# A transformer block in float32 parts: row maxima as one transpose a quad through device memory, and the relu output's high part on GpSimd

## The reference

```
qkv = layernorm(x) @ w_qkv.T + b_qkv           # 16 heads of 16
s   = (q * 0.25) @ k.T + mask                  # rows in 4 blocks of 128
a   = softmax(s) @ v
x1  = x + layernorm(a @ w_out.T + b_out)
h   = relu(layernorm(x1) @ W1 + b1)            # 1024 wide
out = x1 + layernorm(h @ W2 + b2)
```

## Time and profile before

| | us |
|---|---|
| median of 3 runs | 2275.53 (2271.7 to 2275.71) |
| the profiled execution, its own time | 2267.57 |
| its span, first to last instruction | 2265.8 |
| PE busy in the span | 2116.1 (93%) |
| DVE busy | 1567.3 (69%) |
| ACT busy | 1418.0 (63%) |
| POOL busy | 764.4 (34%) |

### The profile page before, as it was taken

How to read it: one execution, slowest core, us unless ns; L and a number is a source line. 1 busy time by engine, 2 the same in 40 slices (tenths; PEclk the granted TensorE clock), 3 DMA queues, 4 the chain that set the end, 5 groups by cost and what they waited for, 6 DMA issues and landing times.

```text
span 2265.8 us, 50967 instructions
## 1 busy us (share of the span) xinstructions
PE 2116.1 (93%) x18432; PEld 1648.0 (73%) x18432; DVE 1567.3 (69%) x3140; ACT 1418.0 (63%) x2437; POOL 764.4 (34%) x1161
## 2 busy tenths in 40 slices
PE   4899999999999999999999999999999999999985
PEld 2577777777777777777777777777777777777765
DVE  5767786667776677776667776677776667776542
ACT  2567666566666666666666666666666666666563
POOL 2033333233233233233233233243233233233234
PEclk8999999999999999999999999999999999999998
DMA  5332343332333323333323333322333323332300
GB/s 132 84 59 64 78 85 69 68 59 62 80 78 70 72 54 69 81 79 71 73 53 69 82 79 70 74 55 67 83 79 70 75 53 70 82 79 61 65 22 20
DMA packets 128931, 158.35 MB, mean 70 GB/s; under 512 B 27617, under 2 KB 78561, under 8 KB 128737
## 3 DMA queue, kind: packets, MB, share of 16 engines
q1 hardware_dynamic: 128208, 155.24, 32.0%
q10 hardware_dynamic: 528, 0.52, 0.1%
HBM read 37.17 MB, written 16.78 MB: 24 GB/s over the span
## 4 chain that ended last, share of the span: by engine, by line
PE 56%; DVE 15%; issue 10%; ACT 8%; POOL 6%; SPq 1%; DMA 1%; DVEq 0%; POOLq 0%; ACTq 0%
PE p_lin L341 17%; PE p_lin L445 14%; PE p_att L326 6%; POOL h_lo L678 5%; PE p_lin L377 5%; DVE neg_max L554 4%; PE p_lin L373 4%; PE p_att L323 4%; PE p_lin L334 3%; PE p_lin L386 2%; ACT h_hi L503 2%; ACT h_f L503 2%; DVE qk L569 2%; PE p_lin L403 2%; DVE x_lo L565 2%
## 5 line engine op out<-in xcount | busy, mean ns | idle before, releaser
L554 DVE TENSOR_REDUCE neg_max<-p_att 128x4 f32<-128x1024 f32 (+1 forms) x640 | 765.5, 1212 | 237.3 <-PE p_att L323 162.6
L472 ACT ACTIVATE probs<-p_att 128x1024 f32<-128x1024 f32 x640 | 635.7, 1027 | 253.6 <-PE p_att L326 158.0
L678 POOL TENSOR_TENSOR h_lo<-h_f,h_hi 128x256 fp32r<-128x256 f32 x512 | 365.1, 737 | 584.6 <-ACT h_hi L503 581.5
L503 ACT ACTIVATE h_f<-p_lin,b_s 128x256 f32<-128x256 f32 x512 | 249.2, 487 | 264.4 <-PE p_lin L341 264.4
L341 PE MATMUL p_lin<-x_hi,w_hi 128*128 128x256 f32 (+1 forms) x1280 | 304.6, 319 | 35.8 <-DVE x_lo L565 19.2
L326 PE MATMUL p_att<-stack 49*128 49x256 f32 (+1 forms) x3072 | 311.8, 304 | 9.6 <-DVE neg_max L554 8.2
L326 PEld LDWEIGHTS p_att<-stack 49*128 49x128 f32 (+1 forms) x3072 | 237.5, 187 | 94.7 <-issue 54.5
L445 PE MATMUL p_lin<-w_hi,h_hi 128*128 128x256 f32 x1024 | 293.0, 286 | 3.4 <-ACT h_hi L503 3.3
L445 PE MATMUL p_lin<-w_lo,h_hi 128*128 128x256 f32 x1024 | 284.1, 277 | 0.0
L445 PE MATMUL p_lin<-w_hi,h_lo 128*128 128x256 f32 x1024 | 283.8, 277 | 0.0
L341 PE MATMUL p_lin<-x_lo,w_hi 128*128 128x256 f32 (+1 forms) x1280 | 283.5, 303 | 0.0
(11 more groups left out here) (77 smaller groups left out, 3196.1 us busy)
## 6 DMA issues: line engine op xcount, KB each, us to landing
stack<-qk SPq DMA_DIRECT2D x1536, 64.0 KB, 2.3
xr<-x SPq DMA_DIRECT2D x32, 512.0 KB, 4.9
out<-yf SPq DMA_DIRECT2D x64, 256.0 KB, 2.5
xa<-x SPq DMA_DIRECT2D x31, 512.0 KB, 3.9
stack<-max_t SPq DMA_DIRECT2D x256, 4.0 KB
probs<-w SPq DMA_DIRECT2D x2, 512.0 KB, 4.8
probs<-w_qkv_t SPq DMA_DIRECT2D x2, 384.0 KB, 5.4
xa<-x ACTq DMA_DIRECT2D x1, 512.0 KB, 4.7
```

The costliest lines, as they stand in the source:

```text
L472: nc.scalar.activation(probs[:, prob_slot(quad, c), :, :], bank("scores", n)[:, :, :], ACT.Exp, scale=SCALE).then_inc(exp_done, 1)
L503: last = nc.scalar.activation(dst, bank("f1", n)[:, u * HALF:(u + 1) * HALF], ACT.Relu, bias=b1_s[:, m:m + 1])
L554: nc.vector.tensor_reduce(dst, src, axis=AX.X, op=ALU.max, negate=True).then_inc(red_done, 1)
L678: last = nc.gpsimd.tensor_tensor(h_parts[1][:, m, :], h_f[:, n % 2, u, :], h_parts[0][:, m, :].bitcast(F32), ALU.subtract)
```

## The change

Four things. `neg_max` is laid out so that all maxima of a quad are 32 neighbouring columns, and `max_t` is one transpose, 128x32 to 32x128. The copy is then 32x128. Since a DMA has to bring 32 rows of 128 into two rows of 2 x 512, the row goes out to a tensor in device memory (`store_row`) and comes back from it (`load_row`), one DMA each; SP waits between them. The relu unit writes `h_f` alone (two activations); GpSimd adds zero to it to round it into the high part (128x512), waits for that, and subtracts (128x512). The wait for `f2` goes from ScalarE to GpSimd. GpSimd's memsets go behind the first two `ln1_rstd`. All five orders are written anew; those of ACT and DVE aren't shown here.

```diff
--- before.py
+++ after.py
@@ ORDER: a new order for each engine; around the changed units, for TensorE, GpSimd and SP @@
     "PE": [
...
+        ("f1", 6, -1), ("f1", 7, -1), ("scores", 15, 0), ("scores_max", 6, 1), ("scores", 16, 0), ("pv", 2, 0),
+        ("scores", 17, 0), ("scores", 18, 0), ("scores_max", 7, 1), ("max_t", 0, 1), ("f2", 2, -1),
+        ("o_t", 2, 0), ("scores", 19, 0), ("scores_max", 8, 1), ("scores_max", 9, 1), ("o2", 0, 0),
+        ("f2", 3, -1), ("pv", 3, 0), ("scores", 0, 1), ("scores", 1, 1), ("scores_max", 10, 1), ("o_t", 3, 0),
...
+        ("x1", 0, 2), ("op", 0, 0), ("scores", 3, 1), ("scores", 4, 1), ("max_t", 1, 1), ("x1", 1, 2),
+        ("op", 1, 0), ("qk", 0, 2), ("qk", 1, 2), ("scores_max", 13, 1), ("scores_max", 14, 1),
+        ("scores", 5, 1), ("qk", 2, 2), ("scores", 6, 1), ("pv", 0, 1), ("scores", 7, 1), ("max_t", 2, 1),
+        ("o_t", 0, 1), ("qk", 3, 2), ("scores", 8, 1), ("scores_max", 15, 1), ("x2", 0, 0), ("x2", 1, 0),
+        ("scores", 9, 1), ("scores_max", 16, 1), ("scores_max", 17, 1), ("scores_max", 18, 1), ("f1", 0, 0),
+        ("f1", 1, 0), ("f1", 2, 0), ("f1", 3, 0), ("scores_max", 19, 1), ("scores", 10, 1),
+        ("scores_max", 0, 2), ("pv", 1, 1), ("scores", 11, 1), ("scores", 12, 1), ("scores_max", 1, 2),
+        ("f2", 0, 0), ("max_t", 3, 1),
...
     "POOL": [
+        ("h_lo", 2, 13), ("h_lo", 3, 13), ("h_lo", 4, 13), ("h_lo", 5, 13), ("h_lo", 6, 13), ("h_lo", 7, 13),
+        ("ln1_rstd", 0, 16), ("lnf_rstd", 0, 13), ("ln1_rstd", 1, 16), ("lnf_rstd", 1, 13),
+        ("final_add", 0, 13), ("final_add", 1, 13), ("lny_rstd", 0, 14), ("lny_rstd", 1, 14), ("x1_add", 0, 14),
+        ("x1_add", 1, 14), ("ln2_rstd", 0, 14), ("ln2_rstd", 1, 14), ("h_lo", 0, 14), ("h_lo", 1, 14),
...
     "SP": [
+        ("store", 1, 10), ("load_stack", 3, 13), ("store_row", 3, 12), ("load_row", 3, 12),
+        ("load_stack", 4, 13), ("store_row", 0, 13), ("load_xr", 0, 12), ("load_row", 0, 13),
+        ("load_stack", 5, 13), ("load_stack", 6, 13), ("load_stack", 7, 13), ("store_row", 1, 13),
+        ("load_xa", 0, 15), ("store", 0, 11), ("load_row", 1, 13), ("load_stack", 0, 14), ("store_row", 2, 13),
+        ("load_stack", 1, 14), ("load_row", 2, 13), ("load_stack", 2, 14),
@@ the row of maxima @@
-        neg_max = sb("neg_max", [P, 2, KB, 2, 2])
-        max_t = sb("max_t", [4, L], F32R)
+        neg_max = sb("neg_max", [P, 2, 2, 2, KB])
+        max_t = sb("max_t", [4 * KB, P], F32R)
+        shift = nc.dram_tensor("shift_rows", [2, 4 * KB, P], F32, kind="Internal").ap()
...
-        row_in = sem("row_in")
+        row_out, row_in = sem("row_out"), [sem(f"row_in{j}") for j in range(2)]
...
+                elif what == "store_row":
+                    ready = b * 8 * QUADS + 16 * (n // 2)
...
+                    wait(sp, ev["max_t"], b, QUADS, n + 1)
+                    if not isinstance(b, int) or ready > 0:
+                        sp.wait_ge(row_in[n % 2], ready)
+                    sp.dma_start(shift[n % 2], max_t[:, :].bitcast(F32)).then_inc(row_out, 16)
                 elif what == "load_row":
-                    wait(sp, ev["max_t"], b, QUADS, n + 1)
-                    for pair in range(2):
-                        sp.dma_start(stack[STACK:STACK + ROW + 1:ROW, 0, 2 * n + pair, :].bitcast(F32),
-                                     max_t[2 * pair:2 * pair + 2, :].bitcast(F32)).then_inc(row_in, 16)
+                    at = slice(STACK, STACK + ROW + 1, ROW)
+                    wait(sp, row_out, b, 16 * QUADS, 16 * (n + 1))
+                    sp.dma_start(stack[at, 0, 2 * n:2 * n + 2, :].bitcast(F32),
+                                 shift[n % 2].rearrange("(s j k) n -> j s (k n)", s=2, j=2)).then_inc(row_in[n % 2], 16)
...
                 if what == "max_t":
                     wait(pe, red_done, b, QC, CH * (n + 1))
-                    for kb in range(KB):
-                        last = nc.tensor.transpose(dst[0:4, kb * P:(kb + 1) * P],
-                                                   neg_max[:, n % 2, kb, :, :].rearrange("p s j -> p (s j)"),
-                                                   ident[:, :])
+                    last = nc.tensor.transpose(dst[0:4 * KB, 0:P],
+                                               neg_max[:, n % 2, :, :, :].rearrange("p s j k -> p (s j k)"),
+                                               ident[:, :])
...
-                    wait(dve, row_in, b, 32 * QUADS, 32 * n)
-                    nc.vector.tensor_copy(max_t[:, :], bank("max_t", n)[0:4, :]).then_inc(ev["max_t"], 1)
+                    wait(dve, row_out, b, 16 * QUADS, 16 * n)
+                    nc.vector.tensor_copy(max_t[:, :], bank("max_t", n)[0:4 * KB, 0:P]).then_inc(ev["max_t"], 1)
@@ the parts of the relu output @@
                 elif what == "relu":
-                    half = n // 4
                     wait(act, mm["f1"], b, 8, n + 1)
                     wait(act, h_lo, b, 8, n - 1)
-                    wait(act, mm["f2"], b, 4, 2 * half)
                     for u in range(2):
                         m = 2 * (n % 4) + u
-                        for dst in (h_f[:, n % 2, u, :], h_parts[0][:, m, :]):
-                            last = nc.scalar.activation(dst, bank("f1", n)[:, u * HALF:(u + 1) * HALF], ACT.Relu,
-                                                        bias=b1_s[:, m:m + 1])
+                        last = nc.scalar.activation(h_f[:, n % 2, u, :], bank("f1", n)[:, u * HALF:(u + 1) * HALF],
+                                                    ACT.Relu, bias=b1_s[:, m:m + 1])
...
                 elif what == "h_lo":
+                    m = 2 * (n % 4)
                     wait(pool, ev["f1"], b, 8, n + 1)
-                    for u in range(2):
-                        m = 2 * (n % 4) + u
-                        last = nc.gpsimd.tensor_tensor(h_parts[1][:, m, :], h_f[:, n % 2, u, :],
-                                                       h_parts[0][:, m, :].bitcast(F32), ALU.subtract)
-                    last.then_inc(h_lo, 1)
+                    wait(pool, mm["f2"], b, 4, 2 * (n // 4))
+                    nc.gpsimd.tensor_tensor(h_parts[0][:, m:m + 2, :].rearrange("p u n -> p (u n)"),
+                                            h_f[:, n % 2, :, :].rearrange("p u n -> p (u n)"),
+                                            zero[:, :].broadcast_to([P, L]), ALU.add).then_inc(h_hi, 1)
+                    wait(pool, h_hi, b, 8, n + 1)
+                    nc.gpsimd.tensor_tensor(h_parts[1][:, m:m + 2, :], h_f[:, n % 2, :, :],
+                                            h_parts[0][:, m:m + 2, :].bitcast(F32), ALU.subtract).then_inc(h_lo, 1)
@@ GpSimd's memsets at the start, moved behind the first two ln1_rstd jobs @@
-            for j in range(2):
-                nc.gpsimd.memset(stack[ROW * j + 32:ROW * (j + 1), 1, :, :].bitcast(F32), 1.0).then_inc(ones_set, 1)
-                pool.wait_ge(ones_set, j + 1)
-            nc.gpsimd.memset(values[:, :, :], 1.0).then_inc(consts, 1)
-            pool.wait_ge(consts, 2)
+            def set_ones():
+                pool.wait_ge(rstd_done["ln1"], 2)
...
+                    if kind == "ln1" and n == 1 and isinstance(b, int) and b == 0:
+                        set_ones()
```

More of the change, by code:

```diff
@@ L18 @@
     "PE": [
-        ("f2", 2, -2), ("scores_max", 4, 0), ("scores", 15, -1), ("scores", 16, -1), ("pv", 2, -1),
-        ("scores", 17, -1), ("scores", 18, -1), ("scores_max", 5, 0), ("max_t", 0, 0), ("f2", 3, -2),
-        ("scores", 19, -1), ("o_t", 2, -1), ("scores_max", 6, 0), ("scores_max", 7, 0), ("scores_max", 8, 0),
-        ("pv", 3, -1), ("v", 0, 0), ("v", 1, 0), ("x1", 0, 1), ("scores", 0, 0), ("scores_max", 9, 0),
-        ("scores", 1, 0), ("o_t", 3, -1), ("x1", 1, 1), ("scores", 2, 0), ("o2", 1, -1), ("qk", 0, 1),
@@ L24 @@
-        ("op", 0, -1), ("op", 1, -1), ("max_t", 1, 0), ("scores", 3, 0), ("scores", 4, 0),
-        ("scores_max", 10, 0), ("qk", 1, 1), ("scores_max", 11, 0), ("scores_max", 12, 0), ("pv", 0, 0),
-        ("scores", 5, 0), ("scores", 6, 0), ("scores_max", 13, 0), ("qk", 2, 1), ("qk", 3, 1), ("scores", 7, 0),
-        ("o_t", 0, 0), ("scores", 8, 0), ("scores_max", 14, 0), ("x2", 0, -1), ("x2", 1, -1), ("scores", 9, 0),
-        ("scores_max", 15, 0), ("scores_max", 16, 0), ("max_t", 2, 0), ("f1", 0, -1), ("f1", 1, -1),
@@ L29 @@
-        ("scores_max", 17, 0), ("f1", 2, -1), ("f1", 3, -1), ("scores", 10, 0), ("scores_max", 18, 0),
-        ("scores_max", 19, 0), ("pv", 1, 0), ("scores", 11, 0), ("scores_max", 0, 1), ("scores", 12, 0),
-        ("f2", 0, -1), ("f2", 1, -1), ("f1", 4, -1), ("f1", 5, -1), ("f1", 6, -1), ("f1", 7, -1),
-        ("scores_max", 1, 1), ("scores", 13, 0), ("o_t", 1, 0), ("max_t", 3, 0), ("scores_max", 2, 1),
-        ("scores", 14, 0), ("scores_max", 3, 1), ("o2", 0, 0),
+        ("scores_max", 2, 1), ("scores_max", 3, 1), ("scores", 13, 0), ("o_t", 1, 0), ("f2", 1, -1),
@@ L56 @@
[L56 to L60 removed]
```

(15 more changed lines are left out.)

62 lines of the change are left out of this document (33 added, 29 removed), and 1 row of the table ORDER.

## The result

The changed kernel takes 2215.71 us (median of 4 runs, 2212.99 to 2219.19), the kernel before 2273.61 us on the same chip (4 runs, 2270.1 to 2275.71). The ratio is 0.9748, 95% interval 0.9728 to 0.9768: 58 us faster, where 27 were forecast. (The text ahead gives the new transpose as 128x32 to 32x128 and the row as 16 KB; the rows show 128x16 to 16x128 and 8 KB, since a quad has 16 maxima a row. The step of the forecast doesn't change.)

What follows compares the result with a forecast made beforehand. TensorE was taken to bound the middle (65.41 of 67.62 us busy), chains through all engines the ends. -42 - 25 + 32 + 6 + 5 - 3 = -27 us; 2267.6 - 27 + 8 = 2249 us, range 2208 to 2290.

Steps and rivals of the forecast that it cites:

- the two stalls' places: First half of a batch: TensorE stalls 0.4 us at the twelfth score unit's bank, 0.6 at f2 0 for h_lo 3.
- Transposes, -42: TensorE, maxima: three of four transposes go, 384 x 0.11 = 42 us saved, 1.31 us a batch.
- Bank waits, -25: TensorE's waits for an f1 bank, 13.6 us before max_t and 10.9 before f1, counted as won.
- GpSimd's pace, +32: f1 groups: GpSimd takes 2.65 us a unit, stalling TensorE 1.0 us a batch in the first half, 32 us.
- I take 1.29: GpSimd's 128x512 add of zero priced at 1.29 us, like the existing 128x512 row; bounds 0.47 and 1.47.
- The forecast's own walk: Unit-by-unit timing from f1 0: h_lo 3 at 13.0 us, needed by f2 0's last quarter at 12.0.
- rival (A): Neither GpSimd's nor the row's stall appears: -42 - 25 + 2 = -65 us, 2211; chance 0.14.
- Row of quad 1, +6: Row through device memory takes 5.7 us against quad 1's 5.6 us gap: 0.2 us a batch charged, 6 us.
- SP's queue, nothing: Stacks waiting behind the row DMAs in SP's queue are used more than 8 us later, so nothing charged.
- Start, -3: Kernel start: memsets behind the first two rstd bring the first transposes 2.6 us sooner.
- End, +5: Last batch: GpSimd's pace delays f2 3's readout from 2257.9 to 2263.2, +5.3 us.
- The last term, +8.0: Added at the end: the shown median, 2275.53 us, lies 8.0 us above the profiled execution's 2267.57.

Runs made afterwards that it cites:

- the row alone: Kernel before, old orders, ScalarE writing the high part as before, with single transpose, row through device memory and later memsets: 2301.49 us, ratio 1.0118.

## Why the prediction was right and wrong
The direction, the bound (TensorE in the middle, chains at the ends) and the two stalls' places were right. The size was off: 27 us forecast, 58 measured. By its steps:

- **Transposes, -42.** Right: 128 rows are left, and putting three of four back costs 45 us.
- **Bank waits, -25.** Right in size: both rows are gone. But only some 9 us of it come from the relu's move, the rest from the new order, which also changed waits that the forecast left as they were (xr, x_lo, the exponential, o_t).
- **GpSimd's pace, +32. This is the step that failed**, by the term "I take 1.29" for the add. The second operand is one column read over and over, and that op takes 1.04 us, not the 1.29 of two full operands; a unit takes 2.36 us, not 2.65. The forecast's own walk with 2.36 gives h_lo 3 at 2.4 + 9.4 = 11.8, before f2 0's last quarter at 12.0, and exp 10 done at 9.1, before 9.3: no stall. The runs with a longer pair show that the walk holds. The bounds of the add (0.47 and 1.47) held its value, and rival (A) named the case, at too small a chance; that its time, 2211, comes so near is partly luck, since it has the ends at +2 where they cost 12.5.
- **Row of quad 1, +6.** Too high: the way out takes 1.4 us for 8 KB instead of 2.5, and the wait appears in 3 of 128 quads, 3.2 us in all. (The 0.2 us for waking the queues stand in no row; in the trace before, SP issues a row 0.02 us behind the copy. The figure of about 2.0 us that the forecast quotes for a small DMA is above the 1.4 measured, too.)
- **SP's queue, nothing.** Right in the new order; that it would be dear elsewhere is shown by the row alone, 26 us of it.
- **Start, -3.** Wrong in sign: the first transposes come at 15.47 instead of 12.1, and the first row goes out at 50.09 instead of 45.74. The move's price, memsets beside VectorE's tensor_scalar, isn't in the sum. With the memsets behind ln1_apply the transposes come at 9.37, 2.7 us sooner, where the forecast had 2.6.
- **End, +5.** Right: 6.0 us measured from the last x2 transposes on, of 8.2 behind the last batch's first row.

With the pace and the row at their measured size, near nothing, the middle reads -42 - 25 = -67 us, against 67 measured over the 31 periods. The ends cost 12.5 instead of 2. So 2267.6 - 67 + 12.5 = 2213 us for a profiled execution; the changed kernel's took 2213.0. The last term, +8.0 from the profiled execution to the median, was 2.7 for the changed kernel (2212.99 to 2215.71): another 5 us. Two things stay open in this sum. The -25 came out right as a net, from other waits than the two it named, as the rows of the waits show. And TensorE's work fell by the 1.3 us a period of the transposes although the tiles' new places cost it up to 0.37, so some 0.4 us of shorter work stand against that. A candidate, which no run tests: each wait also adds to the busy time some 0.16 us, the rest of the matmul that runs out ahead of it (0.28 long against a step of 0.12), and TensorE's listed waits fall from 198 to 142, which by this estimate is 9 us, 0.3 a batch.
